# A graph network kernel on one core: GpSimd's runs of indirect transfers are divided by waits for landing

## What is computed

```python
h = jnp.maximum(_layernorm(x, axis=-1), 0.0)
x = x + _L0_gnn_ref(h, edge_index, edge_weight, ...)   # three GCN convolutions, then a dense product
h = jnp.maximum(_layernorm(x, axis=-1), 0.0)
x = x + _L1_gnn_ref(h, edge_attr_128, ...)             # mean over edges, two dense products with batchnorm
h = jnp.maximum(_layernorm(x, axis=-1), 0.0)
x = x + _L2_gnn_ref(h, edge_index, ...)                # six steps of mean over edges, product, relu
h = jnp.maximum(_layernorm(x, axis=-1), 0.0)
x = x + _L3_gnn_ref(h, edge_index, ...)                # two steps round one GCN convolution, tanh
```

```python
h = x @ W
msg = h[src] * norm[:, None]        # norm = dinv[src] * w * dinv[dst]
out = jax.ops.segment_sum(msg, dst, num_segments=n_nodes)
```

## Time and profile before

| what | value |
|---|---|
| time, median of 3 runs | 3777.04 us (3771.08 to 3794.89) |
| span of the profiled execution, first to last instruction | 3778.5 us |
| time of the profiled execution beside its span | not listed apart |
| mean granted clock of TensorE | 0.826 of full speed |
| instructions | 45814 |

### The profile page before, as it was taken

One profiled execution on the slowest core, in us unless ns is written; L12 is line 12 of the kernel. 1 busy time (PEld: TensorE's weight loads), 2 busy tenths in 40 slices (PEclk: granted clock), 3 DMA queues, 4 the chain that ended last, 5 costly groups with the idle time before them and its releaser, 6 DMA issues. The chain is left out here.

```text
span 3778.5 us, 45814 instructions
## 1 busy us (share of the span) xinstructions
PE 2654.6 (70%) x11055; PEld 1615.7 (43%) x11055; DVE 2151.6 (57%) x7980; ACT 2009.2 (53%) x4381; POOL 1431.0 (38%) x1507
## 2 busy tenths in 40 slices
PE   4666555656666667799999747787787878775641
PEld 2433333434544545554444322454454545443420
DVE  5533254556658856433333466677677777776620
ACT  1555455556556665455555488565666566553400
POOL 5444434442534335100000000546464645444476
PEclk8877777778888888999999858888889888876865
DMA  4544343344445555334334388444454444333210
GB/s 87 148 132 125 103 119 100 95 121 124 123 128 177 165 150 168 123 133 137 135 136 136 128 259 291 136 144 143 133 160 137 152 143 153 120 106 101 82 58 37
DMA packets 528965, 504.90 MB, mean 134 GB/s; under 512 B 58706, under 2 KB 389955, under 8 KB 528616
## 3 DMA queue, kind: packets, MB, share of 16 engines
q1 hardware_dynamic: 477388, 415.73, 34.4%
q0 software_dynamic: 47184, 85.73, 8.7%
q10 hardware_dynamic: 4172, 0.99, 0.1%
HBM read 246.45 MB, written 260.27 MB: 134 GB/s over the span
## 5 line engine op out<-in xcount | busy, mean ns | idle before, releaser
L1839 POOL DMA_INDIRECT h_G<-step_tab,row_i x294 | 282.0, 959 | 470.3 <-DMA step_tab<-l_NR 194.1
L796 PE MATMUL a_PA<-a_H,w 128*128 128x512 f32 x504 | 308.6, 745 | 197.7 <-ACT a_H L960 160.8
L1839 POOL DMA_INDIRECT h_M<-step_tab,row_i x294 | 283.8, 965 | 227.1 <-PE h_P L1944 148.0
L1559 DVE TENSOR_SCALAR b_Y<-b_BP,col 128x512 f32<-128x512 f32 x148 | 109.9, 743 | 354.2 <-PE b_BP L1513 354.2
L1513 PE MATMUL b_BP<-b_Z,w 128*128 128x512 f32 x592 | 266.3, 592 | 0.0
L270 POOL DMA_INDIRECT h_G<-msg_tab,row_i x147 | 142.1, 967 | 318.4 <-PE h_P L306 150.8
L1541 ACT ACTIVATE b_Z<-b_BQ,bn 128x512 f32<-128x512 f32 x148 | 115.0, 777 | 257.2 <-PE b_BQ L1505 256.9
L208 ACT ACTIVATE l_ln_sd<-l_ln_mv,lneps 128x8 f32<-128x8 f32 (+1 forms) x136 | 41.0, 301 | 383.1 <-DVE l_ln_mv L2149 219.6
L2185 DVE TENSOR_TENSOR_SCAN h_T<-keep,h_T,h_P 128x512 f32<-128x512 bf16 x196 | 223.3, 1139 | 35.7 <-issue 18.6
L796 PEld LDWEIGHTS a_PA<-a_H,w 128*128 128x128 f32 x504 | 105.9, 236 | 322.1 <-ACT a_H L960 191.5
L969 ACT ACTIVATE a_H<-a_PA,col 128x512 f32<-128x512 f32 x252 | 163.7, 669 | 140.0 <-PE a_PA L796 87.8
(11 more groups left out here) (384 smaller groups left out, 6730.5 us busy)
## 6 DMA issues: line engine op xcount, KB each, us to landing
b_HI<-hin_tab SPq DMA_DIRECT2D x148, 256.0 KB, 2.8
y_tab<-b_Y SPq DMA_DIRECT2D x148, 256.0 KB, 2.0
l_Y<-y_tab SPq DMA_DIRECT2D x148, 256.0 KB
l_X<-x_tab SPq DMA_DIRECT2D x148, 256.0 KB
x_tab<-a_X SPq DMA_DIRECT2D x112, 256.0 KB
hin_tab<-a_HI SPq DMA_DIRECT2D x112, 256.0 KB
a_XR<-in_x SPq DMA_DIRECT2D x97, 256.0 KB
out_rows<-l_O SPq DMA_DIRECT2D x97, 256.0 KB
```

Source lines behind the costliest of these rows:

```text
L796: nc.tensor.matmul(PA[b][:, 0:nt * P], w[:, :], h[b][:, 0:nt, :].rearrange("p t d -> p (t d)"), start=True, stop=True).then_inc(done, 1)
L1559: nc.vector.tensor_scalar(Y[b][:, :], BP[b][:, :], col[:, C_B12:C_B12 + 1], None, ALU.add).then_inc(b_y, 1)
L1839: pool.indirect_dma_start(out=GR_[i % 2][b][:, k, :], out_offset=None, in_=table[:, :], in_offset=bass.IndirectOffsetOnAxis(ap=row_i[:, t ...
```

## The change

Pool's program is the only one that is touched, and it only waits more. `x_got` counts the landed gathers of a ring buffer, `slots_set` the landed scatters, `xd_got` the landed gathers of `a_XD`, and `slot_got` those of `src_v`; each adds 16 per transfer. `after(engine, sem, n)` waits where n is above zero.

```diff
                 if i:
+                    pool.wait_ge(x_got[s % RING][1], x_need(s, 1))
                     for t in itertools.islice(scatters, NT if i == IT - 1 else 8):
+                        after(pool, slots_set, 16 * (t - t % 4))
                         pool.indirect_dma_start(out=node_tab[:, :], ...).then_inc(slots_set, 16)
@@
                     after(pool, sn.normed, 2 * (i - 2) + b + 1)
                     after(pool, xd_st[i % 2][b], 16 * (i // 2))
+                    if b == 1:
+                        pool.wait_ge(xd_got[i % 2][0], 16 * SUB[0] * (i // 2 + 1))
                     for j in range(nt):
@@
             for i in range(IT):
                 after(pool, wd_set, i - 3)
+                pool.wait_ge(xd_got[i % 2][1], 16 * SUB[1] * (i // 2 + 1))
                 for t in range(first_tile(i, 0), first_tile(i + 1, 0)):
+                    if t == first_tile(i, 1):
+                        pool.wait_ge(slot_got[i % 4], 16 * (sum(SUB) * (i // 4) + SUB[0]))
                     pool.indirect_dma_start(out=src_v[:, t, :], ...).then_inc(slot_got[i % 4], 16)
+                pool.wait_ge(slot_got[i % 4], 16 * sum(SUB) * (i // 4 + 1))
                 if i + 1 < IT:
                     raw(i + 1)
```

## The result

The changed kernel takes 3657.39 us (median of 4 runs, 3649.46 to 3658.76), the kernel before 3778.67 (4 runs): a ratio of 0.9675, 95% interval 0.9651 to 0.9698, 121 us less.

A forecast was written before the change was run, and what follows sets the result against it. Pool's long unbroken runs of transfers were taken to nearly stop the other engines. Gains of 72 (edge steps), 28 (end of chain) and 39 us (first hop) make 139; 3778.5 - 139 - 1.5 = 3638 us, range 3570 to 3735.

The forecast's parts named there:

- (a): Rival: no effect; quiet halves are waits for data and the breaks are hidden; 3775 to 3790 us, chance 0.06.
- limit of 9 to 12 us of unbroken issue: Pool's runs: beyond roughly this length of unbroken issue the other engines nearly stop until the run is over.
- Edge steps, 72 us: Edge steps 3 to 13: two breaks a step bring the period from 32.2 to 25 us, ten times; ends 22 and 95.
- joined runs of 11: Edge steps: the last 4 scatters and next 7 gathers may join, 13.9 us, so some stopping stays.
- The end of the chain, 28 us: 402 to 499 us: breaks in the run of 37 stay hidden; about 35 us at stake, 28 taken, ends 0 and 35.
- First hop, 39 us: 499.4 to 859.07 us: 359.7 becomes 320.4, eleven iterations at 25.0 us with Pool near pace-setter; ends 0 and 53.
- 3 us or more as a sign of being wrong: Pool's idle time before the broken groups: about 2 us expected; at this length the forecast is wrong.
- The tail: First hop from the last raw on: 45.4 us, kept unchanged in the sum; quicker only in the upper end of 53.
- The start, put at 0 +-5: Kernel before 80 us, a run of 38 transfers: no gain or loss, within 5 us.
- (b): Rival: partial gain; stops return in runs of 11, landing nearer 3.0, Pool paces the hop at 28; about 3715, chance 0.24.
- (c): Rival: slower; the stop follows transfers lately issued and persists while breaks lengthen the loop; 3837 us at half price, chance 0.07.
- (d): Rival: more gain; engines run at undisturbed 10 to 12 us a step, Pool alone paces; 183 us, 3594, chance 0.13.

The follow-up runs named there:

- e5: The changed kernel with three small memsets on Pool in place of each wait for landing (before each fifth scatter too), stopping chip: 3589.02 us, 0.9646 of the kernel before.
- e1: Only the waits of the edge steps (parts 1 and 2 of the diff), against the kernel before on a non-stopping chip: 3329.04 us, ratio 1.0165.
- e2: Only the waits in raw and src_v of the first hop (parts 3 and 4), against the kernel before on a non-stopping chip: 3357.15 us, ratio 1.0252.
- e4: Changed kernel, but each group of transfers waits only for the group before the previous one, at most 8 in flight; non-stopping chip: 3273.54 us, 0.9993 of before.
- e7: Repetition of the kernel with at most 8 transfers in flight and no pause, again on a non-stopping chip: 3270.08 us, ratio 0.9988 to the kernel before.
- e9: Pauses at all the places of the change, one memset each instead of three; non-stopping chip: 3280.12 us, ratio 1.0021 to the kernel before.

## Why the prediction was right, and where it was off

The forecast was 3638 us, range 3570 to 3735, faster; measured 3657. Of its 139 us, 121 came.

**What bounds the kernel: shown, and only on this kind of chip.** That unbroken issue by Pool stops the other engines there was read from coincidence, and the prediction said that no row gives the cause. e5 is the test: nothing but a pause at the same places, 0.9646, and the waits for "remote" of the first hop go from 154.5 us to 3.0. Rival (a), that the quiet halves are waits for data and the breaks are hidden, falls with it. The Trainium skill, page "SBUF — State Buffer", section "Who interferes with whom", says that only the port pair shared by DVE and GpSimd contends and that "PE and ACT never wait on anyone". On the stopping chips the trace disagrees with the second: ACT stands 10.2 us with its input ready, though whether at a port or at something else is not shown. On the non-stopping chips the traces agree: in e1 PE is busy 7.51 of 8.60 us beside seven transfers. There (a)'s 0 us would even be too good, since the breaks cost. The prediction's limit of 9 to 12 us of unbroken issue did not hold: in the instance above ACT stands from 213.4 on, 5.6 us into the run, and the runs of 7 show stops as well.

**Edge steps, 72 us: 65.6.** Period 25.6 where I took 25, but by another sum, so the closeness is in part luck. The forecast had Pool at 22.7 and the engines at up to 24 as the slower side. In the trace Pool paces: over the ten periods it waits 13.9 us for the ring (none in e1). Its breaks are longer than the 2.05 us taken: 28.6 / 10 = 2.9 before the fifth scatter, and some 2.8 before the first. With 15 transfers in 19.2 us, and 0.30 of each break already in them, that makes 19.2 + 2.6 + 2.5 = 24.3 us, and 1.4 of waiting for the ring. The joined runs of 11 were named as the place where stopping would stay, and it did: the one with the instance above is nearly empty in its later part.

```profile
207.80:213.00 5.20, 5.20 (x45) 4.91 (x45) 3.43 (x17) 4.66 (x12) 3.96 (x5) 1.00 0.57 166
213.00:221.50 8.50, 0.37 (x4) 0.13 (x2) 0.80 (x2) 0.00 (x0) 6.67 (x7) 0.72 0.71 182
```

An empty stretch alone is not proof of a stop: e1, on the non-stopping chip, has one too in a run of 11, where the engines have run out of work. DVE waits there for the gather itself, 10.88 us, and PE for what follows from it:

```profile
270.90:279.40 8.50, 0.00 (x0) 0.00 (x0) 0.87 (x4) 0.00 (x0) 6.65 (x7) 0.62 0.18 46
```
```profile
277.23 0.87 DVE L193 BATCH_NORM_STATS2 a_ln_st<-a_XR 128x6 f32<-128x128 f32 x4 [10.88 <-DMA a_XR<-in_x,src_i]
```

What tells the two apart is the releaser: "remote", with the input long there, or a transfer that has only now landed.

**The end of the chain, 28 us: 29.1, the number by luck.** The prediction had Pool's 37 transfers with their breaks at 64 us and hidden. In the trace they are not hidden: from the gather of step 13 to `raw(2)` each of Pool's waits is for its own transfers or for "issue", the last of them 1.78 us for `src_v`, so the 68.3 us are Pool's own. The gain is the 97.4 us of before less these 68.3, not the share of the engines' stop that the 28 stood for. In e5, whose breaks are shorter, the stretch takes 65.2, and its last wait is again for the store of `a_XD` (2.38 us).

**First hop, 39 us: 20.7 in the eleven iterations, and 22.5 behind them.** This is the step whose size failed twice, in opposite directions. By the prediction's own marks (499.38 to the `a_X` at 859.07, now 414.10 to 731.26) 359.7 us became 317.2, 42.5 less, close to 39 because the two cancel. The mechanism held (Pool becomes the pace-setter). The term was 14 transfers + 4 x 1.75 = 24.5, taken as 25.0; it is 26.7, because the landing was read from one place in a later hop and used for all four breaks. Behind four x rows by destination it is 4.3 us and not 2.05; e2 has 49.5 / 12 = 4.1 on another chip. The upper end of 3.0, the widest that the rows before gave, did not hold that break either, though the sum of the four (10.1 us in e2, where 3.0 each makes 12) lies within. The prediction had named 3 us or more as a sign of being wrong; it was met at this one break of the four. The tail, 45.4 us from `raw(13)` to the `a_X` at 859.07, was carried over unchanged, "with the tail quicker as well" only as an upper end; it fell to 23.6 (707.68 to 731.26). That was a gain left out of the sum.

**The start, put at 0 +-5: +9.4, outside.** The landing of the first 4 scatters, which stand behind the load of `keep`, took 14 us; the new wait made Pool stand for it:

```profile
45.16 1.00 POOL L720 DMA_INDIRECT node_tab<-own_v,end_i  x1 [0.30 <-issue]
60.12 0.98 POOL L720 DMA_INDIRECT node_tab<-own_v,end_i  x1 [13.96 <-DMA node_tab<-own_v,end_i]
```

The prediction named what is queued behind the scatter (the next gathers) and not what the scatter itself is queued behind. That the wait for landing is what costs is shown by e5, which has pauses at the same places and starts edge step 3 at 80.2, as before. That the load of `keep` is the reason for the 14 us is argued from its place one instruction ahead, not tested.

**Rivals (b), (c), (d).** The edge steps and the hop's iterations ended between (b)'s and the forecast's. (d)'s mechanism, Pool alone pacing, is what the trace shows in both stages, but its price is excluded, since Pool's own pace is 25.6 and 26.7 and not 22.7 and 24.5. (c), that the breaks lengthen the loop and the stop persists, did not come true on a stopping chip. Its outcome does on a non-stopping one, by a simpler way: there is nothing to win, and the breaks are paid in full, 53 us in e1 and 81 in e2. The prediction had no case "another chip"; its 0.07 for slower was a chance for the chip that the traces were taken on.

**What stays open.** Why some chips stop and others don't, and what holds an engine whose input is there; whether the length of unbroken issue or the number of transfers in flight is what counts (e4 and e7 were made for that and met no stopping chip; e5 has both a pause and, by it, fewer in flight); how short a pause may be (e9); and the whole changed kernel was not run on a non-stopping chip, so 53 + 81 is a sum of two runs, not a measurement.

The change wins back only the smaller part of what the stopping chips lose. Behind hop 1, where nothing was changed, they lose another 240 us: 3648 - 753 = 2895 us to the end in the changed kernel, 3348 - 694 = 2654 in e2. By Pool's marks all of it lies where Pool gathers and scatters: from hop 1 to the last gather of messages 647 against 543, then 827 against 825 to the first gather of the six steps, then 1409 against 1274 to the last scatter. That is where the waits for "remote" are, and that no such wait and no loss lies in the 825 us between ties both to Pool's transfers. The durations of single instructions explain little of it. In the stretch without transfers they are equal, as for this group of the changed kernel and of e4:

```profile
L1521 PE MATMUL b_BP<-b_Z,w 128*128 128x512 f32 x592 | 266.3, 592 | 0.0
```
```profile
L1529 PE MATMUL b_BP<-b_Z,w 128*128 128x512 f32 x592 | 266.3, 593 | 0.0
```

DVE's and ACT's largest groups agree within 1% (the scan `h_T` 1139 ns in the changed kernel and in e2, `a_H` 669 and 668). PE's are longer on the stopping chip elsewhere, `a_PA` 724 ns against 647 in e2, at a mean granted clock of 0.837 against 0.871; whether the lower clock follows from the stops was not tested.

## What to carry to other kernels

When several engines go quiet together for the later part of a long burst of GpSimd's indirect transfers, first see whether they had work: an engine whose input was ready and that started only behind the burst was stopped, one that waited for a landing was not. Then try a pause in the burst before a wait for landing: it gave 0.9646 where the waits gave 0.9747 on the same chip, and its cost is known beforehand. If a wait is used, read the landing time for the kind of transfer that is waited for, and look at what it is queued behind. Look at the bursts of the rest of the program too: those behind the changed part, left as they were, lose 240 us, twice what the change won. Run the kernel before on more than one chip before calling such a wait a gain: what is 3% faster on one was, by its two halves, 1.6% and 2.5% slower on another.

## What the runs showed of the hardware that was not expected

The kernel before takes 3725 and 3779 us on two occasions and 3272 to 3276 us on four others (medians), with durations of DVE's and ACT's instructions that agree within 1% and equal issue by Pool (7 transfers in 6.60 us). On the slow ones engines stand still beside Pool's indirect transfers with their input ready, ACT for 10.2 us in the instance above; on the others no trace shows a single such wait. In the first hop the difference is whether PE executes 1 or 56 instructions beside seven transfers, and there a pause of 2.0 us after 3 or 4 transfers is enough to keep the engines going. Four gathers of 128 rows of 512 bytes took 4.1 to 4.3 us on average to land behind the last one's issue, groups of 8-byte elements 1.7 to 1.9, on both kinds of chip.
